# A mixture-of-experts stage from all experts on all tokens to three groups dense and five groups sorted by expert

## The chip, the cores and the metric

The kernel runs on one core of a Trainium2 chip. The metric is the device time of one execution in microseconds (us). All arithmetic of the path is in float32, except some counts in bf16.

## The reference

A decoder of two layers on x of 32 batches x 128 tokens x 128 channels, with a context of 32 x 77 x 128. The six blocks are the kernel's six stages; the third is the one that changes. Cut to what matters:

```python
x = x + _L0_attn_ref(_layernorm(x), ...)           # stage 1
x = x + _L0_xattn_ref(_layernorm(x), ctx, ...)     # stage 2
x = x + _L0_ffn_ref(_layernorm(x), ...)            # stage 3, below
x = x + _L1_attn_ref(_layernorm(x), ...)           # stage 4: 16 heads of 8, a bias by position
x = x + _L1_xattn_ref(_layernorm(x), ctx, ...)     # stage 5
x = x + _L1_ffn_ref(_layernorm(x), ...)            # stage 6: 16 experts, top 1

def _L0_ffn_ref(x, norm_weight, gate_w, w1, b1, w2, b2):     # 8 experts, hidden 256, top 2
    t = x * rsqrt(mean(x * x) + 1e-6) * norm_weight
    gate_logits = t @ gate_w.T
    gate_scores, expert_idx = top_k(gate_logits, 2)
    combine = zeros(T, 8).at[..., expert_idx].add(softmax(gate_scores))
    for W1, B1, W2, B2, c in experts:
        out += c[:, None] * (gelu(t @ W1.T + B1) @ W2.T + B2)
    return x + out
```

In the reference each expert is applied to every token, and six of the eight weights `c` of a token are zero.

## The kernel before

One program on the five engines, with semaphores written out by hand. Each stage has a function per engine (`by_tensor`, `by_vector`, `by_scalar`, `by_gpsimd`, `by_sync`), which issues that engine's instructions in a fixed order; an engine runs them in that order and waits where a `wait_ge` says so. x (`core.x`) stays in SBUF, tokens in the partitions. Batches are taken in groups of G = 4 (512 tokens); there are 8 groups. Stages overlap at their edges: a stage's `following` issues the next one's opening ("norm", "flip", "keys", "queries").

Stage three before is a loop over the groups (`turn(i, more)`), dense: for each group VectorE norms twice (a layer norm, then the RMS norm; `norm`, parts 1 to 4, spread between the experts of the group before), TensorE flips the tokens (L1857), computes logits (L1864), and then for each of 8 experts two hidden matmuls of 128 x 512 (L1872) and 8 output matmuls of 128 x 128 (L1880; each float32 matmul is two instructions in the trace). ScalarE applies GELU (L1732), VectorE adds the output times `combine` into `total` (L1833), and `route` finds the two best experts. GpSimd adds `total` to x (L1695). At its start GpSimd writes a tile of zeros (L1706), and SyncE clears a DRAM tensor of 16 regions x 4096 rows x 128 (`sorted_dram`, eight DMAs, L1676) which stage six uses.

Stage four is attention over the 32 batches, a software pipeline of one batch a step: TensorE scores (L1487), VectorE adds the bias (L1363) and takes the peak (L1377), GpSimd subtracts it (`lower`, L1199) and forms the keys by head for the next batch (`own_of`, L1190), ScalarE exponentiates (L1288), TensorE flips (L1498) and weighs (L1514), VectorE divides and adds to x. Every fourth step a new group is normalised: VectorE's moments (`moments_of`, which calls `before.x_of`), GpSimd's `rstd_of` (L1175 to L1184, with the power L1180), ScalarE's `xn_of` (L1246).

Stages five and six: `fourth_done` makes every engine wait, before stage five, for all of stage four's x and for `regions_cleared`. In stage six each token goes to one of 16 experts. During stage five `Routing` finds the expert and the rank of each token, and GpSimd writes the rows to the region of their expert in `sorted_dram` by indirect DMAs (L2642, 128 rows each). Then tiles of 128 rows of one expert are loaded by SyncE (L2794), flipped (L3039), multiplied with the weights of the tile's owner (L3053), whose number TensorE loads into a register, flipped (L3061), multiplied again (L3069), stored (L2804), and gathered by indirect DMAs (L2825). Four tiles are a quad.

## Time and profile before

| | |
|---|---|
| median of 3 runs | 1601.73 us (1600.66 to 1601.9) |
| the profiled execution | 1602.82 us, span 1601.0 us |
| TensorE busy | 94% of the span |
| VectorE, ScalarE, GpSimd busy | 60%, 52%, 37% |
| stage three (first logits to stage four's first queries) | 567.20 to 822.26 us |
| stage four's last x, start of stage five | 1047.94 us |

The span is from the first to the last instruction of the execution that was profiled; its own time is beside it. Busy times of engines overlap. A wait names the instruction that came last before it.

### The profile page before, as it was taken

To read this page: it belongs to the slowest core of one execution; us is meant where nothing else is said; L and a number is where in the kernel's file an instruction comes from. 1 tells how busy PE (TensorE), PEld (TensorE's weight loads), DVE (VectorE), ACT (ScalarE), POOL (GpSimd) and SP (SyncE) were. 2 spreads that over 40 slices of the span, in tenths; PEclk is the share of its full clock that TensorE was granted. 3 is DMA by queue.
4 is the path that set the end of the run, shared out by engine and by line. 5 is a ranking of instruction groups with operands and counts; after the bars stand their busy time and mean duration, and the time that the engine had idled before them with its cause. 6 is when DMAs were issued, how large, how long until landed. Compare 5 with 4: busy or idle time off the path is not lost.

```text
span 1601.0 us, 39392 instructions
## 1 busy us (share of the span) xinstructions
PE 1501.8 (94%) x15207; PEld 1146.3 (72%) x15207; DVE 959.2 (60%) x2605; ACT 832.8 (52%) x1574; POOL 588.7 (37%) x583
## 2 busy tenths in 40 slices
PE   6999999996999999999979999969999999998998
PEld 5777777765777767777756666647888888885765
DVE  3343444346788746655549999846666676675223
ACT  4545554445776634333347777625555655543431
POOL 4243445423222111111047878623333444444024
PEclk9999999998999999999999999979999999999999
DMA  5021230000000089400000000000000000000323
GB/s 153 16 61 29 73 108 7 12 1 5 11 10 6 7 303 384 153 0 0 0 1 2 2 2 2 2 12 2 6 6 8 11 13 7 9 7 31 97 74 88
DMA packets 76527, 68.85 MB, mean 43 GB/s; under 512 B 19533, under 2 KB 57034, under 8 KB 76234
## 3 DMA queue, kind: packets, MB, share of 16 engines
q1 hardware_dynamic: 74314, 62.36, 12.1%
q0 software_dynamic: 2048, 4.20, 0.8%
q8 instruction: 115, 1.88, 0.5%
q14 instruction: 50, 0.41, 0.1%
HBM read 24.58 MB, written 41.96 MB: 42 GB/s over the span
## 4 chain that ended last, share of the span: by engine, by line
PE 65%; issue 11%; POOL 10%; DVE 8%; ACT 4%; SPq 1%; DMA 1%; POOLq 0%; DVEq 0%; ACTq 0%
PE bank L1880 7%; PE bank L1872 7%; PE bank L2368 5%; PE bank L2400 5%; PE bank L2362 4%; PE bank L2379 4%; POOL s_p L1199 4%; PE bank L1498 3%; PE bank L1514 3%; PE bank L2391 3%; PE bank L853 2%; PE bank L3025 2%; PE bank L873 2%; PE bank L3014 2%; PE bank L826 2%
## 5 line engine op out<-in xcount | busy, mean ns | idle before, releaser
L1295 ACT COPY s_pT<-bank 77x512 f32<-77x512 f32 (+1 forms) x256 | 134.8, 585 | 71.7 <-PE bank L1498 71.4
L2190 POOL TENSOR_TENSOR s_p<-s_p,s_inverse 128x616 f32<-128x616 f32 x64 | 78.4, 1229 | 229.6 <-DVE s_inverse L2313 229.6
L1732 ACT ACTIVATE s_hT<-bank,w_s_b 128x512 f32<-128x512 f32 x128 | 87.3, 687 | 126.3 <-PE bank L1872 125.2
L1498 PE MATMUL bank<-ident,s_p 128*77 128x128 f32 (+1 forms) x1024 | 138.1, 281 | 12.3 <-ACT s_p L1288 10.5
L1498 PEld LDWEIGHTS bank<-ident,s_p 128*77 128x77 f32 (+1 forms) x1024 | 114.1, 146 | 40.2 <-ACT s_p L1288 22.5
L1880 PEld LDWEIGHTS bank<-w_s_w2T,s_hT 128*128 128x128 f32 x1024 | 122.3, 192 | 26.8 <-issue 15.3
L1199 POOL TENSOR_TENSOR s_p<-s_p,s_peak 128x1024 f32<-128x1024 f32 x64 | 120.1, 1898 | 30.2 <-DVE s_peak L1377 30.2
L1880 PE MATMUL bank<-w_s_w2T,s_hT 128*128 128x128 f32 x1024 | 124.4, 276 | 2.2 <-ACT s_hT L1732 2.2
L1288 ACT ACTIVATE s_p<-s_p 128x616 f32<-128x616 f32 (+1 forms) x128 | 111.4, 892 | 25.3 <-POOL s_p L1199 20.9
L1872 PE MATMUL bank<-s_ln_xnT,w_s_w1T 128*128 128x512 f32 x256 | 121.7, 604 | 0.0
L1833 DVE SCALAR_TENSOR_TENSOR s_total<-bank,s_combine,s_total 128x128 f32<-128x128 f32 x256 | 72.1, 344 | 74.6 <-PE bank L1880 73.2
L2297 DVE TENSOR_REDUCE s_peak<-bank 128x8 f32<-128x616 f32 x64 | 50.7, 792 | 88.4 <-PE bank L2379 88.4
L719 DVE TENSOR_TENSOR s_aT<-bank,s_weight 128x512 f32<-128x512 f32 x64 | 44.2, 691 | 98.7 <-PE bank L863 82.3
L2368 PE MATMUL bank<-pos_bias,s_ctx 128*32 128x128 f32 x3072 | 91.3, 274 | 0.6 <-issue 0.6
L2362 PE MATMUL bank<-s_ctx,s_kq 128*128 128x308 f32 x256 | 89.0, 440 | 1.9 <-ACT s_kT L2222 1.8
L2241 ACT ACTIVATE s_p<-s_p 128x616 f32<-128x616 f32 x64 | 46.6, 728 | 81.9 <-DVE s_p L2301 81.8
L1363 DVE TENSOR_TENSOR s_p<-bank,pos_bias 128x1024 f32<-128x1024 f32 x64 | 77.6, 1217 | 17.2 <-PE bank L1487 17.2
L2368 PEld LDWEIGHTS bank<-pos_bias,s_ctx 128*32 128x32 f32 x3072 | 82.1, 110 | 5.4 <-issue 1.6
L711 DVE TENSOR_TENSOR s_weight<-s_decay,bank 128x512 f32<-128x512 f32 x64 | 41.0, 682 | 73.4 <-ACT s_decay L559 73.4
L565 ACT COPY s_qT<-bank 128x512 f32<-128x512 f32 x64 | 37.5, 586 | 85.3 <-PE bank L826 85.3
L1190 POOL TENSOR_TENSOR w_s_q<-w_s_oT,w_s_lane_of 128x308 f32<-128x308 f32 (+1 forms) x64 | 55.2, 872 | 69.8 <-ACT w_s_oT L1261 32.3
L1487 PE MATMUL bank<-w_s_q,w_s_oT 32*128 32x308 f32 (+1 forms) x512 | 63.5, 566 | 16.2 <-POOL w_s_q L1190 12.5
(302 smaller groups left out, 3449.3 us busy)
## 6 DMA issues: line engine op xcount, KB each, us to landing
sorted_tokens<-s_zero SPq DMA_DIRECT2D x8, 4096.0 KB, 29.5
s_rows<-sorted_tokens SPq DMA_DIRECT2D x48, 64.0 KB, 1.9
routed_tokens<-s_routed SPq DMA_DIRECT2D x12, 256.0 KB, 2.4
x_all<-x SPq DMA_DIRECT2D x8, 256.0 KB, 3.1
w_s_gateup<-s_gateup SPq DMA_DIRECT2D x1, 2048.0 KB
out<-x_all SPq DMA_DIRECT2D x8, 256.0 KB
w_s_k<-ctxT SPq DMA_DIRECT2D x8, 154.0 KB, 2.2
s_ctx<-ctxT SPq DMA_DIRECT2D x8, 154.0 KB, 2.4
```

What stands on the lines that cost most here:

```text
L1199: nc.gpsimd.tensor_tensor(part, part, peak[:, b % 2, HU * u:HU * (u + 1)].unsqueeze(2).to_broadcast([P, HU, keys]), ALU.subtract).then_inc ...
L1288: nc.scalar.activation(part, part, ACT.Exp).then_inc(exp_ready, 1)
L1295: nc.scalar.copy(pT[0:keys, b % 2, 4 * q:4 * q + 4, :].rearrange("m h t -> m (h t)"), bank[0:keys, flip_bank("p", b, q), :]).then_inc(drai ...
L1363: nc.vector.tensor_tensor(p[:, b % 2, HU * u:HU * (u + 1), :].rearrange("p h m -> p (h m)"), scores_at(u).rearrange("p g c -> p (g c)"), b ...
L1498: last = nc.tensor.transpose(bank[0:keys, into, j * T:(j + 1) * T], p[:, b % 2, 4 * q + j, :], core.ident[:, :])
L1732: nc.scalar.activation(hT[:, e % 2, c, :], bank[:, HIDDEN + k % 4, :], ACT.Gelu, bias=w.s3_b1[:, k:k + 1]).then_inc(hT_ready, 1)
L1872: nc.tensor.matmul(bank[:, HIDDEN + k % 4, :], w.s3_w1T[:, k * P:(k + 1) * P], ln.xnT[:, :], start=True, stop=True).then_inc(hidden_done, 1)
L1880: last = nc.tensor.matmul(bank[:, OUT[e % 2], n * D:(n + 1) * D], hT[:, e % 2, c, n * T:(n + 1) * T], w.s3_w2T[:, e * CHUNKS + c, :], star ...
L2190: nc.gpsimd.tensor_tensor(part, part, inverse[:, b % 2, heads].unsqueeze(2).to_broadcast([P, HU, M]), ALU.mult).then_inc(share_ready, 1)
L2362: nc.tensor.matmul(bank[:, into, 0:GM].rearrange("p (n m) -> p n m", m=M), kq[:, h, :], ctx[:, g % 3, :, 0:M], start=True, stop=True).then ...
L2368: last = nc.tensor.matmul(bank[lane:lane + LANE, into, tile * D:(tile + 1) * D], ctx[:, g % 3, b % G, row:row + LANE], vo[:, QUAD * q + he ...
L2400: last = nc.tensor.matmul(bank[:, OUT, 0:D], pT[:, b % 2, j, :], values(b, j // PER_QUAD)[:, j % PER_QUAD, :], start=(j == 0), stop=(j == ...
```

## The change

Stage three is written anew. Groups 0, 1 and 2 (`DENSE`) are computed as before, by all eight experts, in 24 units of one expert on one group, `UNITS3`. The tokens of groups 3 to 7 go to two experts each. The routing of all groups runs beside the 24 units: `STARTS3` says at which unit a group starts, and its phases follow slot by slot (0 moments and scales, 1 norm, 2 flip, 3 logits, 4 route, 5 combine or count of rows ahead, 6 offset or rank, 7 to 10 dispatch). A count by matmul gives each row its rank; GpSimd writes each token's row twice, by indirect DMAs, into the regions of its two experts in DRAM (40 DMAs of 128 rows). VectorE's `settle` works out once where the tiles of each expert stand. Then 48 tiles (12 quads) of rows of one expert are loaded, flipped, multiplied with W1 as the moving operand and the rows stationary, biased on VectorE (`add_biases`, b1 spread over all partitions), passed through GELU on ScalarE, flipped (8 flips a quad), multiplied with W2, biased (`keep_routed`) and stored. In stage four GpSimd gathers two rows for each token (`gather`, 40 indirect DMAs in steps 3 to 22), and VectorE multiplies them by the token's shares and adds them to x (`add_results`, eight instructions a group, inside `moments_of`).

The norms are also new: one set of moments gives the scales of both norms (GpSimd, `scales_of`), and ScalarE writes the tokens and replaces x by x plus its layer norm (`normalise`, eight activations a group), so that only the experts' sum is added later. Where the regions are cleared is changed too: at the start only the 8 x 2560 rows of stage three, and the whole of `sorted_dram` again, for stage six, once stage four's gathers have landed. Stage six's semaphores for dispatch and gather are fewer, its work is the same.

```diff
...
+                before.gather(pool, b)
...
+DENSE = 3
+SORTED = GROUPS - DENSE
+TILES3 = SORTED * G * 2 + E3
+QUADS3 = TILES3 // G
+REGION3 = SORTED * GT
+CLEARINGS3 = 4
+FLIGHTS = 4
+TOKENS = 6
+UNITS3 = DENSE * E3
+STARTS3 = {3: 0, 1: 1, 4: 3, 5: 5, 6: 7, 7: 9, 2: 10}
+ORDER3 = [0] + sorted(STARTS3, key=lambda g: STARTS3[g])
+COUNTED, SETTLED = 14, 15
...
     def by_sync(sp):
         sp.wait_ge(zero_ready, 1)
+        cleared_rows = sorted_dram[0:E3 * REGION3, :].rearrange("(k p j) d -> k p (j d)", p=P, k=CLEARINGS3)
+        for k in range(CLEARINGS3):
+            sp.dma_start(cleared_rows[k].rearrange("p (r c) -> p r c", c=GT),
+                         zero[:, :].unsqueeze(1).to_broadcast([P, E3 * REGION3 * D // CLEARINGS3 // P // GT, GT])
+                         ).then_inc(cleared, 16)
+        sp.wait_ge(gap_ready, 1)
+        for tile, source in ((b1_all, a["s3_b1"]), (b2_all, a["s3_b2"].rearrange("e d -> (e d)"))):
+            sp.dma_start(tile[:, :], source.unsqueeze(0).to_broadcast(tile.shape)).then_inc(biases_landed, 16)
+        def load(q):
+            for n in range(q * G, (q + 1) * G, 2):
+                pair = nc.sync.value_load(pairs_index[0:1, n // 2:n // 2 + 1], min_val=0, max_val=ALL_ROWS ** 2 - 1)
+                for k, tile in enumerate((pair & (ALL_ROWS - 1), pair >> ALL_ROWS.bit_length() - 1)):
+                    sp.dma_start(rows[:, (n + k) % (FLIGHTS * G), :],
+                                 tiles_dram[bass.ds(tile & (ALL_ROWS - 1), 1), :, :].rearrange("k p d -> p (k d)")
+                                 ).then_inc(rows_landed[q % FLIGHTS], 16)
+        sp.wait_ge(pairs_ready, 1)
+        for g in range(DENSE, GROUPS):
+            sp.wait_ge(dispatched[g - DENSE], G * 2 * 16)
+        for g in range(DENSE):
+            sp.wait_ge(filled, turn["xnT", g] + 1)
+        for q in range(FLIGHTS):
+            load(q)
+        for q in range(QUADS3):
+            if q + FLIGHTS < QUADS3:
+                sp.wait_ge(filled, turn["rows", q] + 1)
+                load(q + FLIGHTS)
+            sp.wait_ge(out_used, UNITS3 + q + 1)
+            sp.dma_start(done_dram[q * GT:(q + 1) * GT, :].rearrange("(n p) d -> p n d", p=P),
+                         routed[:, q % 2, :, :]).then_inc(routed_stored[q % 2], 16)
...
+        for k in range(2):
+            sp.wait_ge(gathered[k], (SORTED + 1 - k) // 2 * G * 2 * 16)
         cleared_rows = sorted_dram.rearrange("(k p j) d -> k p (j d)", p=P, k=CLEARINGS)
         for k in range(CLEARINGS):
             sp.dma_start(cleared_rows[k].rearrange("p (r c) -> p r c", c=GT),
...
+        def dispatch(g, n):
+            b = (g - DENSE) * G + n
+            if n == 0:
+                if g == DENSE:
+                    pool.wait_ge(cleared, CLEARINGS3 * 16)
+                pool.wait_ge(ranking_v, ranked_links(g) + RANKED)
+                pool.wait_ge(tokens_ready, G * (nth(g) + 1))
+            for k in range(2):
+                nc.gpsimd.indirect_dma_start(
+                    out=sorted_dram[:, :], out_offset=bass.IndirectOffsetOnAxis(ap=slot_index[:, b, k:k + 1], axis=0),
+                    in_=tokens_of(g)[:, n, :], in_offset=None).then_inc(dispatched[g - DENSE], 16)
...
+        for k in range(UNITS3):
+            if group_in(k, 0) is not None:
+                scales_of(group_in(k, 0))
+            for n in range(G):
+                if group_in(k, 7 + n) in range(DENSE, GROUPS):
+                    dispatch(group_in(k, 7 + n), n)
+            if k % E3 == 1 and k > E3:
+                add_total(k // E3 - 1)
+        add_total(DENSE - 1)
+        following.by_gpsimd(pool, "norm")
+        following.by_gpsimd(pool, "keys")
...
+    def gather(pool, step):
+        g, n = (step + 9) // G, (step + 9) % G
+        if g not in range(DENSE, GROUPS):
+            return
+        j, b = g - DENSE, (g - DENSE) * G + n
+        if (j, n) == (0, 0):
+            pool.wait_ge(done_ready, 1)
+            for k in range(2):
+                pool.wait_ge(routed_stored[k], QUADS3 // 2 * 16)
+        if j >= 2 and n == 0:
+            pool.wait_ge(added, 2 * (j - 1))
+        for k in range(2):
+            nc.gpsimd.indirect_dma_start(
+                out=rows[:, j % 2 * 2 * G + 2 * n + k, :], out_offset=None, in_=done_dram[:, :],
+                in_offset=bass.IndirectOffsetOnAxis(ap=done_index[:, b, k:k + 1], axis=0)).then_inc(gathered[j % 2], 16)
+    def add_results(dve, g):
+        j = g - DENSE
+        dve.wait_ge(gathered[j % 2], (j // 2 + 1) * G * 2 * 16)
+        dve.wait_ge(x_normed, GROUPS)
+        for k in range(2):
+            if k:
+                dve.wait_ge(added, 2 * j + 1)
+            for n in range(G):
+                x = core.x[:, g * G + n, :]
+                last = nc.vector.scalar_tensor_tensor(
+                    out=x, in0=rows[:, j % 2 * 2 * G + 2 * n + k, :], scalar=share[:, g * G + n, k:k + 1], in1=x,
+                    op0=ALU.mult, op1=ALU.add)
+            last.then_inc(added, 1)
+        dve.wait_ge(added, 2 * j + 2)
...
+        def normalise(g):
+            i = nth(g)
+            act.wait_ge(shifts_ready, i + 1)
+            if i >= TOKENS:
+                earlier_g = ORDER3[i - TOKENS]
+                act.wait_ge(filled, turn["xnT", earlier_g] + 1)
+                if earlier_g >= DENSE:
+                    act.wait_ge(dispatched[earlier_g - DENSE], G * 2 * 16)
+            for n in range(G):
+                nc.scalar.activation(tokens_of(g)[:, n, :], core.x[:, g * G + n, :], ACT.Identity,
+                                     bias=shifts[:, i % 2, 1, n:n + 1],
+                                     scale=scales[:, i % 2, 1, n:n + 1]).then_inc(tokens_ready, 1)
+            act.wait_ge(tokens_ready, G * (i + 1))
+            for n in range(G):
+                x = core.x[:, g * G + n, :]
+                last = nc.scalar.activation(x, x, ACT.Identity, bias=shifts[:, i % 2, 0, n:n + 1],
+                                            scale=kept[:, i % 2, n:n + 1])
+            last.then_inc(x_normed, 1)
...
+        def output_of_tiles(q, owned):
+            u = UNITS3 + q
+            pe.wait_ge(drained, turn["hidden", q, CHUNKS - 1] + 1)
+            pe.wait_ge(out_used, u - 1)
+            for n in range(G):
+                for c in range(CHUNKS):
+                    last = nc.tensor.matmul(bank[:, OUT[u % 2], n * D:(n + 1) * D], hT[:, u % 2, c, n * T:(n + 1) * T],
+                                            w.s3_w2T[:, bass.ds(owned[n] * CHUNKS + c, 1), :], start=(c == 0),
                                             stop=(c == CHUNKS - 1))
             last.then_inc(expert_done, 1)
...
+        for k in range(UNITS3):
+            if group_in(k, 2) is not None:
+                flip_tokens(group_in(k, 2))
+            if group_in(k, 3) is not None:
+                logits_of(group_in(k, 3))
+            if group_in(k, 5) is not None:
+                (flip_combine if group_in(k, 5) < DENSE else count_ahead)(group_in(k, 5))
+            if k == COUNTED:
+                count_all()
+            if k == 0:
+                hidden_of(0)
+            if k + 1 < UNITS3:
+                hidden_of(k + 1)
+            if group_in(k, 6) in range(DENSE):
+                offset_of(group_in(k, 6))
+            output_of(k)
+        pe.wait_ge(owners_ready, 1)
+        flip_rows(0)
+        flip_rows(1)
+        now = owners_of(0)
+        hidden_of_tiles(0, now)
+        for q in range(QUADS3):
+            if q + 1 < QUADS3:
+                later = owners_of(q + 1)
+                hidden_of_tiles(q + 1, later)
+            if q + 2 < QUADS3:
+                flip_rows(q + 2)
+            if q:
+                output_of_tiles(q - 1, past)
+            if q == QUADS3 - 1:
+                following.by_tensor(pe, "opened")
+            flip_hidden(q)
+            if q == QUADS3 - 2:
+                core.wait_set_back(pe)
+                pe.wait_ge(drained, turn["hidden", q, CHUNKS - 1] + 1)
+                following.by_tensor(pe, "flip")
+                following.by_tensor(pe, "keys")
+            past, now = now, later
+        output_of_tiles(QUADS3 - 1, past)
+        pe.wait_ge(out_used, UNITS3 + QUADS3 - 1)
+        following.by_tensor(pe, "queries")
...
```

`x_of(engine, g)` of stage three waits for `x_ready` in groups 0 to 2 and calls `add_results` in the others. `QUADS3` is 12.

## Rows read from the trace of the kernel before

**Rows 1.** The page: busy us, share of the span, instructions of each engine.
```profile
PE 1501.8 (94%) x15207; PEld 1146.3 (72%) x15207; DVE 959.2 (60%) x2605; ACT 832.8 (52%) x1574; POOL 588.7 (37%) x583
```
**Rows 2.** Timeline of TensorE in stage three: start us, us, what [idle before].
```profile
567.20 1.87 PE L1864 MATMUL bank<-w_s_gateT,s_ln_xnT 128*128 128x8 f32 x8 [0.77 <-ACT s_ln_xnT L1716]
...
601.13 0.96 PE L1864 MATMUL bank<-w_s_gateT,s_ln_xnT 128*128 128x8 f32 x8
...
621.19 1.95 PE L1880 MATMUL bank<-w_s_w2T,s_hT 128*128 128x128 f32 x16
...
624.69 1.95 PE L1880 MATMUL bank<-w_s_w2T,s_hT 128*128 128x128 f32 x16
...
632.20 0.96 PE L1864 MATMUL bank<-w_s_gateT,s_ln_xnT 128*128 128x8 f32 x8
...
822.26 1.02 PE L1468 MATMUL bank<-w_s_v,w_s_q 128*128 128x512 f32 x2
```
**Rows 3.** Busy time in a stretch of stage four: PE, PEld, DVE, ACT, POOL.
```profile
900.00:940.00 40.00, 37.51 (x558) 26.23 (x557) 37.86 (x61) 29.14 (x48) 31.18 (x26) 1.00 0.01 2
```
**Rows 4.** Timeline of GpSimd in stage four and at its end.
```profile
880.84 1.01 POOL L1180 TENSOR_TENSOR s_rstd<-s_variance,minus_half 128x4 f32<-128x4 f32 x1
...
896.02 3.75 POOL L1199 TENSOR_TENSOR s_p<-s_p,s_peak 128x1024 f32<-128x1024 f32 x2 [2.31 <-DVE s_peak L1377]
902.39 1.04 POOL L1190 TENSOR_TENSOR w_s_q<-w_s_oT,w_s_lane_of 128x512 f32<-128x512 f32 x1 [2.62 <-ACT w_s_oT L1261]
...
976.12 3.75 POOL L1199 TENSOR_TENSOR s_p<-s_p,s_peak 128x1024 f32<-128x1024 f32 x2 [2.32 <-DVE s_peak L1377]
...
1047.94 1.06 POOL L2124 MEMSET s_ctx<- 128x1152 f32 x1 [8.86 <-DVE x_all L1403]
```
**Rows 5.** Timeline of TensorE in stage six: counts of rows ahead, then a quad.
```profile
1459.83 0.22 PE L2695 MATMUL bank<-s_chosen,s_ones 128*128 128x48 bf16 x3
...
1498.67 1.89 PE L3053 MATMUL bank<-w_s_gateup,s_rowsT 128*128 x8
1500.40 0.60 PE L3039 MATMUL bank<-ident,s_rows 128*128 128x128 f32 x4
1500.84 1.06 PE L3069 MATMUL bank<-w_s_down,s_hiddenT 128*128 x8
...
1502.17 1.89 PE L3053 MATMUL bank<-w_s_gateup,s_rowsT 128*128 x8
```
**Rows 6.** Timeline of ScalarE: the norm's activations of a group of four.
```profile
803.48 1.65 ACT L1246 ACTIVATE w_s_v<-x_all,s_shift,s_rstd 128x128 f32<-128x128 f32 x4 [6.75 <-POOL s_shift L1184]
```
**Rows 7.** VectorE's busy time in three stretches: route, rank, moments of a group.
```profile
602.46:605.03 2.57, 2.43 (x20) 1.00 1.03 386
1461.24:1462.12 0.88, 0.77 (x5) 1.00 0.00 0
613.80:615.14 1.34, 1.30 (x10) 1.00 1.03 388
```
**Rows 8.** Timeline of SyncE in stage six: two stores, four loads between them.
```profile
1503.29 0.42 SPq L2804 DMA_DIRECT2D routed_tokens<-s_routed  x1
...
1508.11 0.43 SPq L2804 DMA_DIRECT2D routed_tokens<-s_routed  x1
```
**Rows 9.** The line of the indirect DMAs: ns min/median/max, first and last start.
```profile
L2642 POOL DMA_INDIRECT sorted_tokens<-w_s_oT,s_slot_index x32: 953/1057/1215, 1234.8 to 1472.7; - x32
```
**Rows 10.** Timeline of GpSimd: the gap from one indirect DMA to the next.
```profile
1470.17 0.96 POOL L2642 DMA_INDIRECT sorted_tokens<-w_s_oT,s_slot_index  x1 [0.30 <-issue]
```
**Rows 11.** The page's DMA issues: count, KB each, median us to landing.
```profile
sorted_tokens<-s_zero SPq DMA_DIRECT2D x8, 4096.0 KB, 29.5
```
**Rows 12.** A stretch in stage three: busy times, clock, DMA share, GB/s.
```profile
580.00:600.00 20.00, 20.00 (x124) 15.22 (x124) 12.09 (x55) 7.45 (x11) 2.42 (x4) 1.00 1.03 383
```
**Rows 13.** Timeline of VectorE: eight multiply-adds of 128 x 128.
```profile
611.60 2.29 DVE L1833 SCALAR_TENSOR_TENSOR s_total<-bank,s_combine,s_total 128x128 f32<-128x128 f32 x8
```
**Rows 14.** A line of GpSimd in stage one, a sum of 128 x 512: ns min/median/max.
```profile
L510 POOL TENSOR_TENSOR s_z<-s_z,w_s_b x8: 1265/1688/1697, 83.8 to 368.6; 128x512 f32<-128x512 f32 x8
```

More of the change, by code:

```diff
@@ new lines, in by_scalar @@
+        keep_rows(0)
+        keep_rows(1)
+        gelu_of_tiles(0)
+        for q in range(QUADS3):
+            if q + 2 < QUADS3:
+                keep_rows(q + 2)
+            if q + 1 < QUADS3:
+                gelu_of_tiles(q + 1)
+            keep_hidden(q)
+            if q == 6:
+                core.wait_set_back(act)
+                following.by_scalar(act, "norm")
+            if q == QUADS3 - 2:
+                following.by_scalar(act, "flip")
+                following.by_scalar(act, "keys")
@@ L1796, in route, with link @@
             for n in range(G):
+                last = nc.vector.bn_aggr(moments[:, i % 2, n, :], stats[:, n, :])
+            last.then_inc(moments_ready, 1)
+        def route(g):
+            links = routed_links(g)
+            def link(instruction):
+                nonlocal links
+                links += 1
+                instruction.then_inc(routing_v, 1)
+                dve.wait_ge(routing_v, links)
+            batches = slice(g * G, (g + 1) * G)
+            dve.wait_ge(drained, turn["logits", g] + 1)
+            for n in range(G):
@@ L1958, in stage3, with x_of @@
+    def x_of(engine, g):
+        if g < DENSE:
+            engine.wait_ge(x_ready, g + 1)
+        else:
+            add_results(engine, g)
+    LAST = UNITS3 + QUADS3
+    after = After(x_of=x_of, memory=lambda engine: engine.wait_ge(core.set_back, 1),
+                  score_banks=lambda pe: pe.wait_ge(biased, QUADS3),
+                  work_bank=lambda pe: pe.wait_ge(out_used, LAST), gather=gather)
     return Opening(None, by_gpsimd, by_scalar, by_vector, by_tensor, main), after
```

804 lines of the change are left out of this document (544 added, 260 removed).

## The prediction

> **What bounds the kernel now.** I read the page first, then the waits, then the timelines of TensorE, VectorE, ScalarE and GpSimd in stages three, four and six. TensorE is busy for 94% of the span and no other engine for more than 60% [rows 1]. That average hides two regimes.
>
> Stage three runs from its first logits at 567.20 to the first query projection of stage four at 822.26, 255.1 us [rows 2]. It is TensorE work laid end to end: a group of four batches takes 632.20 - 601.13 = 31.07 us, an expert 624.69 - 621.19 = 3.50 us. So eight experts take 28.0, and flips, logits and offset 3.07.
>
> Stage four is different. TensorE and VectorE are both about 94% busy and GpSimd 78% [rows 3], but the chain goes again and again through GpSimd's `lower`. Four steps take (976.12 - 896.02) / 3 = 26.7 us. GpSimd's own work in them is 4 x 3.75 for `lower`, 4 x 1.04 for `own` and 1.6 for the norm of which the power is 1.01, about 20.7 us; the rest of 26.7, 6.0, it waits, 2.3 and 2.6 of it at one `lower` and one `own` [rows 4]. That slack is what the change spends.
>
> **Stage three after: the dense part.** 24 units instead of 64: 24 x 3.50 = 84.0. Three whole groups add 3 x 3.07 = 9.2. The other five still need a flip (0.44, [rows 5]), logits (about 0.8 of the 0.96 shown in [rows 2]), and a count of rows ahead, whose five small bf16 matmuls get 0.2 (three take 0.22 in stage six [rows 5]): 7.2. The pipe's filling, now in the 6.5 us that 255.1 has over eight groups, gets 2.0. Together 102.4.
>
> To this come stalls, as each engine now does a group every two slots. ScalarE takes the norms over: 8 activations a group, four in 1.65 us [rows 6], behind the GELUs of the slot, while TensorE's next slot opens with the flip of these very tokens. Laid out slot by slot, the flip is late by 1.7 and 1.2 us for the first two groups (an offset copy stands ahead there) and by 0.5 for the next three. For group 7, VectorE has route, rank and moments in one slot, of which today's forms take 2.6, 0.9 and 1.3 us [rows 7]; then GpSimd's scales, with a power over twice the columns of today's 1.01, about 2.7 in all: 2.3 late. Group 2 is the eighth to be normalised and there are six token buffers, so its norm waits until all dispatches of group 3 have landed, and these stand in GpSimd's queue behind the scales of groups 6, 7 and 2. The last lands some 19 us after slot 9 starts; TensorE wants the flip at 14.5 and the tokens take 1.65 more: 6.2 late. Sum 12.9, so the dense part is 115.3; 102.4 if none is exposed.
>
> VectorE needs 6.0 and 1.2 us in two slots of some 8.7, so it follows. `settle`, once, is covered by the two output banks.
>
> **The sorted part.** 5 x 4 x 2 + 8 = 48 tiles, 12 quads. Stage six has the same pipeline and prices the steps: a quad takes 1502.17 - 1498.67 = 3.50 us, of it 1.73 for four tile matmuls of 256 columns, 0.44 for a flip of four, 0.89 for the output [rows 5]. Here the output has two chunks (1.78) and the hidden flip is twice as long (0.88): 1.73 + 0.44 + 1.78 + 0.88 = 4.83, times 12: 58.0. SyncE issues four loads and a store in 1508.11 - 1503.29 = 4.8 us [rows 8]: as much, so it may set the pace by a little. VectorE needs about 2.2 for eight adds and as much for register work, which no row of before shows on VectorE. I take the TensorE figure; with VectorE or SyncE as the bound I allow 5.2 to 6.0, that is 4 to 14 us more.
>
> Entry: GpSimd has 20 pairs of dispatches. An indirect DMA takes 0.95 to 1.22 us [rows 9]; I take 1.03, and 0.30 until the next [rows 10], a pair 2.6. Sixteen pairs are left some 17 us after slot 9; they end near 60, and with landing and two quads' loads the rows are there at 71, where TensorE would be ready at 67.5: 3 us, then 1.5 for the copy of the rows and 0.8 for the first biased hidden, and 2.4 at the exit. 7.7 together. With the flip and keys of stage four, 1.3, stage three is 115.3 + 58.0 + 7.7 + 1.3 = 182.3: **72.8 saved**. Bounds: 89 (no stall in either part) and 55 (quads of 6.0, indirect DMAs of 1.5).
>
> The small clearing (10.5 MB) starts at GpSimd's memset in the tail of stage two and at 383 GB/s [rows 12] takes 27 us: it is over before the first dispatch. The two bias broadcasts run behind it unseen.
>
> **Stage four: the gathers.** Two indirect DMAs follow `lower` in each of steps 3 to 22. Behind them in GpSimd's queue stand the next `own`, for which the scores wait, and the next `lower`, for which the exponentials wait. Four steps then hold 20.7 + 8 x 1.33 = 31.3 us of GpSimd's work against 26.7: the 6.0 of waiting is used up and 4.6 is left, five times: **23**. The least is 5 x (8 x 1.25 - 6.0) = 20; the most, with no waiting used, 53. I stay near the least, since the gathers fall where GpSimd waits now. VectorE gets eight more multiply-adds in four steps, 2.3 us [rows 13], on 25.2 of 26.7; beside 31.3 they are covered, except after step 23, where no gather is left: 1.5. Sum 24.5.
>
> **From stage four to five: the clearing.** The eight DMAs of 4096 KB [rows 11] move. They ran at the start of stage three beside the experts; at 383 GB/s, all 16 engines full [rows 12], 33.6 MB take 87.6 us, with start and landing 88.9. Now SyncE issues them only when the last gather, that of step 22, has landed, and every engine enters stage five only when they are complete. In the trace `lower` of step 22 ends at 979.87 and stage five begins at 1047.94 [rows 4], 68.1 later. After the change the pair takes 2.7 of issue and lands 2.3 later, so the clearing ends 5.0 + 88.9 = 93.9 after that `lower`; the stage ends 68.1 + 2.7 + 1.5 = 72.3 after it. All engines stand for **22** us (17 to 26). By the Trainium skill (DMA: Bandwidth & Descriptors, Specifications) a core gets some 358 GB/s of HBM, which would make the clearing 94 us, an estimate, and the wait 28; the trace's 383 is above that and decides.
>
> **Sum.** -72.8 + 24.5 + 22 = -26.3. The profiled execution took 1602.82 us beside its span of 1601.0, so 1576.5; the median of the runs is 1601.73, 1.1 lower: **1575 us**. 0.2%, 3 us, is what a measurement can tell from no change.
>
> **Rivals.**
> - *Stage three without the stalls* (0.15). ScalarE uses some 7.5 of 8.7 us in two slots, so there is room if the shifts come early. -89 + 24.5 + 22 = -42.5: 1559. Against it: the six buffers are a fixed wait behind a full queue.
> - *The wait before stage five does not show* (0.07). -48.3: 1553. It needs a last gather 22 us earlier or a tail of stage four that much longer, and the rate in [rows 12] speaks against it.
> - *VectorE's adds hold GpSimd up* (0.14). The 40 multiply-adds of the gathered rows read two tiles in SBUF while GpSimd lowers scores. If GpSimd stands still for all of them, 5 x 2.3 = 11 us more: 1587. This would be the rule of the Trainium skill (GPSIMD Engine Reference, Specifications): GpSimd's SBUF interfaces are shared with VectorE, with contention when a VectorE instruction has two SBUF inputs. In this trace one and the same GpSimd sum takes 1.27 us at the least and 1.69 in the median [rows 14], so something of the kind may be real.
> - *Slower: the indirect DMA costs more under load* (0.12). The rows are of a GpSimd with little beside it. Each microsecond more for one costs 40 us in stage four, and 32 in stage three, where the dispatches already end last: 72. From 26.3 / 72 = 0.37 us more, 1.70 for each, the gain is gone; at 1.8 the time is 1609. The longest in the trace, 1.22 and the gap of 0.30 [rows 9, 10], would give 1588.
> - The forecast itself has 0.52, its own range 1563 to 1589.
>
> The range 1556 to 1598 leaves out the hidden wait below and the slower case above, 2 in 10. Faster 0.85, within 0.2% 0.03, slower 0.12.
>
> **What will show it.** Dense slots with a gap of about 6 us at the flip of group 2; quads of 4.8 to 5.2 us; stage three near 182 us. In stage four, four steps in 31 us with GpSimd above 95% busy for steps 3 to 22, then 26.7 again. A hole of some 22 us on all engines ahead of stage five's folding, with DMA at 383 GB/s under it. Wrong would be: quads above 6 us (register work on VectorE), GpSimd still idle between gathers, or indirect DMAs above 1.5 us.

## The result and the profile after

The changed kernel took 1609.16 us in the median of five runs (1606.01 to 1611.02), the kernel before 1601.9 beside it (1600.66 to 1604.11). The ratio is 1.0043, 95% interval 1.0028 to 1.0058: slower, where 1575 had been forecast. The profiled execution took 1611.02 us with a span of 1609.1, against 1602.82 and 1601.0: 8.1 more, where 26.3 less was expected.

The page of the kernel after: the engines, and the chain that ended last.
```profile
PE 1445.7 (90%) x14805; PEld 1111.7 (69%) x14805; DVE 928.6 (58%) x2414; ACT 835.0 (52%) x1618; POOL 662.8 (41%) x678
...
PE 59%; issue 14%; DVE 10%; POOL 7%; ACT 6%; DMA 1%; another core or an unknown queue 1%; SPq 1%; DVEq 0%; POOLq 0%; ACTq 0%
```
TensorE has 56 us less to do than in [rows 1], but stands still for 64 us more, and 14% of the chain (11% before) is "issue", time in which nothing that the profile shows was waited for. The timeline of TensorE in the dense part, the sorted part and at stage four's first queries shows where:
```profile
569.05 1.85 PE L2294 MATMUL bank<-w_s_gateT,s_dense_xnT 128*128 128x8 f32 x8 [0.43 <-DVE x_all L1404]
...
629.86 1.39 PE L2287 MATMUL bank<-ident,s_tokens 128*128 128x128 f32 x4 [1.05 <-ACT s_tokens L1963]
...
643.49 1.54 PE L2287 MATMUL bank<-ident,s_tokens 128*128 128x128 f32 x4 [8.73 <-ACT s_tokens L1963]
...
646.96 3.76 PE L2345 MATMUL bank<-s_dense_xnT,w_s_w1T 128*128 128x512 f32 x4
...
669.90 0.94 PE L2357 MATMUL bank<-w_s_w2T,s_hT 128*128 128x128 f32 x6
671.77 0.27 PE L2357 MATMUL bank<-w_s_w2T,s_hT 128*128 128x128 f32 x1 [0.93 <-issue]
...
675.32 0.37 PE L2357 MATMUL bank<-w_s_w2T,s_hT 128*128 128x128 f32 x1 [1.04 <-issue]
...
682.40 0.81 PE L2357 MATMUL bank<-w_s_w2T,s_hT 128*128 128x128 f32 x3 [1.76 <-issue]
...
707.08 1.04 PE L2365 MATMUL bank<-ident,s_tokens 128*128 128x128 f32 x8
...
719.91 1.89 PE L2380 MATMUL bank<-w_s_w1T,s_rowsT 128*128 x8
...
724.74 1.89 PE L2380 MATMUL bank<-w_s_w1T,s_rowsT 128*128 x8
...
772.49 1.02 PE L1469 MATMUL bank<-w_s_v,w_s_q 128*128 128x512 f32 x2
```
Stage three takes 772.49 - 569.05 = 203.4 us, 51.7 less than in [rows 2] where 72.8 was forecast. The dense part, up to the flip of rows at 707.08, takes 138.0 for 115.3; the sorted part 65.4 for 67.0, its quads 4.83 us to the hundredth. Group 2's flip waits 8.7 us, and the four matmuls at 646.96 take 3.76 us behind it instead of 1.88: the granted clock is 0.50 there, TensorE's lower level (1.2 GHz), after it had stood still. Then comes something that no step of the prediction had, called the hole below: from 670 to 683 us the output matmuls come one in about 1.4 us. The profile names "issue" as the releaser, which means that it shows nothing waited for. The two stretches (TensorE, its weight loads, VectorE, ScalarE, GpSimd, granted clock, DMA share, GB/s):
```profile
644.00:648.00 4.00, 3.73 (x18) 2.75 (x18) 0.00 (x0) 2.97 (x9) 3.09 (x4) 0.50 0.18 55
...
670.00:683.00 13.00, 4.12 (x16) 3.34 (x17) 2.00 (x8) 0.34 (x1) 7.41 (x8) 0.57 0.15 45
```
In the hole only GpSimd works. ScalarE stands too, though the matmuls that release its copy are recorded as done at 669.97 (668.82 and 1.15, in TensorE's timeline):
```profile
682.66 0.58 ACT L2006 COPY s_total<-bank 128x512 f32<-128x512 f32 x1 [13.73 <-remote]
```
"remote" says that the profile found no release near its start. GpSimd's timeline, the first and the last of sixteen dispatches that follow each other without a pause:
```profile
659.64 0.96 POOL L1882 DMA_INDIRECT sorted_tokens<-s_tokens,s_slot_index  x1 [5.94 <-DVE s_slot_index L2163]
...
678.59 0.96 POOL L1882 DMA_INDIRECT sorted_tokens<-s_tokens,s_slot_index  x1 [0.30 <-issue]
```
Stage four runs from 772.49 to its last output and then waits; SyncE's timeline and a stretch beside it show for what (TensorE's rows first, of before and of after):
```profile
1047.07 0.49 PE L1524 MATMUL bank<-w_s_o,s_oT 128*128 128x128 f32 x2 [1.40 <-DVE s_oT L1395]
1049.69 0.50 PE L2152 MATMUL bank<-w_s_qT,w_s_kT 64*128 64x128 f32 x4 [2.14 <-DVE w_s_o L2134]
```
```profile
1033.22 0.49 PE L1525 MATMUL bank<-w_s_o,s_oT 128*128 128x128 f32 x2 [1.40 <-DVE s_oT L1396]
1056.62 0.80 PE L2697 MATMUL bank<-w_s_qT,w_s_kT 64*128 64x128 f32 x4 [22.91 <-DVE w_s_o L2679]
```
```profile
965.07 71.44 SPq L1846 DMA_DIRECT2D sorted_tokens<-s_zero  x8
```
```profile
1040.00:1050.00 10.00, 0.00 (x0) 0.00 (x0) 0.00 (x0) 0.00 (x0) 0.00 (x0) 0.50 1.03 389
```
From the first queries to the last output it was 1047.07 - 822.26 = 224.8 us and is 260.7: 35.9 more, forecast 24.5. From there to stage five's folding it was 2.6 and is 23.4: the wait for the clearing is 20.8 us, forecast 22. The opening is 1.8 us later, the rest about 1. So -51.7 + 35.9 + 20.8 + 1.8 + 1.3 = +8.1.

Two questions for the experiments: what fills the 23 us of the dense part that were not forecast, and why stage four pays 36. In stage four VectorE's eight additions for a group stand in a block, beside GpSimd's lowering:
```profile
865.92 3.80 POOL L1199 TENSOR_TENSOR s_p<-s_p,s_peak 128x1024 f32<-128x1024 f32 x2
```
```profile
867.61 2.25 DVE L1947 SCALAR_TENSOR_TENSOR x_all<-s_tokens,s_share,x_all 128x128 f32<-128x128 f32 x2 [0.17 <-DMA s_tokens<-routed_tokens,s_done_index]
```
```profile
L1947 DVE SCALAR_TENSOR_TENSOR x_all<-s_tokens,s_share,x_all x40: 339/347/1981, 834.4 to 969.8; 128x128 f32<-128x128 f32 x40
```
Most of the forty take 0.35 us (minimum, median, maximum in ns), but one in each block takes 1.98. The second of the two shown ends at 869.86, 0.14 behind GpSimd's sum.

### The profile page after: what moved, and what is told of

Its sections match the earlier page's. It is cut to its first block, busy times and chain, and to the rows that moved or that the text cites. A ratio compares the mean times of both kernels' runs of the same rounds, so it can differ in the third digit from the quotient of the medians.

```text
span 1609.1 us, 38896 instructions
## 1 busy us (share of the span) xinstructions
PE 1445.7 (90%) x14805; PEld 1111.7 (69%) x14805; DVE 928.6 (58%) x2414; ACT 835.0 (52%) x1618; POOL 662.8 (41%) x678
## 3 DMA queue, kind: packets, MB, share of 16 engines
q1 hardware_dynamic: 93034, 80.71, 15.5%
## 4 chain that ended last, share of the span: by engine, by line
PE 59%; issue 14%; DVE 10%; POOL 7%; ACT 6%; DMA 1%; another core or an unknown queue 1%; SPq 1%; DVEq 0%; POOLq 0%; ACTq 0%
PE bank L2913 5%; PE bank L2945 5%; PE bank L1515 5%; PE bank L1499 4%; PE bank L2907 4%; PE bank L2924 4%; PE bank L2936 3%; PE bank L853 2%; PE bank L3566 2%; PE bank L873 2%; POOL s_p L1199 2%; PE bank L3555 2%; PE bank L826 2%; PE bank L2345 2%; PE bank L3557 2%
## 5 line engine op out<-in xcount | busy, mean ns | idle before, releaser
L1499 PE MATMUL bank<-ident,s_p 128*77 128x128 f32 (+1 forms) x1024 | 141.5, 285 | 14.5 <-ACT s_p L1289 10.6
L1515 PE MATMUL bank<-s_pT,s_v 77*32 77x128 f32 (+1 forms) x2048 | 73.6, 287 | 21.5 <-DVE x_all L1404 20.4
L1515 PEld LDWEIGHTS bank<-s_pT,s_v 77*32 77x32 f32 (+1 forms) x2048 | 55.8, 114 | 44.6 <-issue 32.5
L1515 PE MATMUL bank<-s_pT,s_ones 77*32 77x128 f32 (+1 forms) x2048 | 78.5, 285 | 2.9 <-issue 2.8
L2924 PE MATMUL bank<-s_kT,s_xnT 128*128 128x308 f32 x256 | 72.9, 426 | 5.9 <-ACT s_xnT L2760 5.4
L853 PEld LDWEIGHTS bank<-s_level,w_band 128*128 128x128 f32 x512 | 59.6, 191 | 26.2 <-issue 19.7
```

The costliest lines, as they stand in the source:

```text
L853: last = nc.tensor.matmul(bank[:, LEVEL + j, c * H1 * TB:(c + 1) * H1 * TB], w.band[:, start:start + T], level[:, b % 2, a, :, :].rearrang ...
L1499: last = nc.tensor.transpose(bank[0:keys, into, j * T:(j + 1) * T], p[:, b % 2, 4 * q + j, :], core.ident[:, :])
L1515: last = nc.tensor.matmul(bank[LANE * r:LANE * (r + 1), WORK, at_column:at_column + T], of_lane(r, j), pT[0:keys, b % 2, LANES * r + j, :] ...
L2924: last = nc.tensor.matmul(bank[:, SCORE5 + q, 0:QUAD * M].rearrange("p (h m) -> p h m", m=M), xnT[:, n * T:(n + 1) * T], kT[:, g % 2, QUAD ...
```

## The experiments

Kernels that leave work out (e4, e6 to e8, e13, e14, e17) and the repeats e15 and e18 ran once each. The kernel before, run beside every set, took 1600.2 to 1601.7 us in the median wherever it ran.

**The clearing moved (e1, e2).** Stage three gets a DRAM tensor of its own, so the clearing for stage six waits for nothing.
```diff
+    sorted3_dram = nc.dram_tensor("sorted_tokens3", [E6 * REGION, D], F32, kind="Internal").ap()
...
-        for k in range(2):
-            sp.wait_ge(gathered[k], (SORTED + 1 - k) // 2 * G * 2 * 16)
-        cleared_rows = sorted_dram.rearrange("(k p j) d -> k p (j d)", p=P, k=CLEARINGS)
+        cleared_rows = later_dram.rearrange("(k p j) d -> k p (j d)", p=P, k=CLEARINGS)
```
e1 issues it behind stage three's last store, e2 behind the bias broadcasts, beside the dense part.

> Stage three gets a sorted tensor of its own in DRAM; the eight clearing DMAs of the tensor of stage six (33.6 MB) no longer wait for the gathers and are issued behind stage three's last store, near 773 us. Theory one (the 21 us in which every engine stands before stage five are this transfer's place in the order, and nothing else waits there): the folding of stage five starts some 21 us earlier, span 1609 - 21 = 1588, if the gathers (64 KB each, from 796 us on) are not held up by the transfer beside them. Rival A: the gathers share the 16 DMA engines with the transfer until about 860; each then lands several us later, GpSimd or VectorE wait for them, and 5 to 10 us of the gain are lost: 1593 to 1598. Rival B: the wait before stage five has another cause, and the time stays at 1609.

> As e1_own_late, but the eight DMAs are issued right behind the two bias broadcasts, near 585 us, so that they run beside the dense part until about 675. Theory one: the wait before stage five goes, 1588, but the dispatches (from 618 us on, 64 KB each) share the DMA engines with the transfer; if they land late, the token buffers of group 2 and SyncE's first loads come later. I expect 0 to 5 us of loss, 1588 to 1593. Rival: the unforeseen hole in TensorE near 670 to 683 us is a lack of instructions whose fetch queues behind DMA traffic; then the hole grows to 20 us or more or comes earlier, stage three takes 210 us or more, and the time is 1595 to 1605. If DMA traffic has nothing to do with it, the hole keeps its 12.5 us.

e1 took 1591.56 us (1582.84 to 1594.78; ratio 0.9933, 0.9904 to 0.9962), e2 1594.24 (0.9957, 0.9943 to 0.9971). In e1's timeline of TensorE the folding follows stage four as before the change:
```profile
1033.52 0.49 PE L1525 MATMUL bank<-w_s_o,s_oT 128*128 128x128 f32 x2 [1.40 <-DVE s_oT L1396]
1036.14 0.81 PE L2695 MATMUL bank<-w_s_qT,w_s_kT 64*128 64x128 f32 x4 [2.14 <-DVE w_s_o L2677]
```
The wait is that transfer's place in the order and nothing else. The gain in time is 17.6 us against the changed kernel's 1609.16, and 21.2 between the two profiles. A little of rival A is there too: with the transfer beside it (e1, e10 to e12, e16) stage four takes 261.4 to 262.7 us, in the four profiles of the changed kernel 258.4 to 260.7. For e2 a stretch beside the transfer, and the hole:
```profile
600.00:640.00 40.00, 31.99 (x198) 23.22 (x196) 25.64 (x157) 24.04 (x57) 21.88 (x36) 0.95 1.04 385
...
670.00:683.00 13.00, 4.78 (x20) 3.53 (x19) 2.00 (x9) 0.12 (x1) 7.67 (x8) 0.64 0.19 60
```
The DMA engines were full until about 670 us, TensorE went on, and the hole came when they were free; it kept its length. What grew is group 2's wait, 12.7 us for 8.7: dispatches land later beside a full transfer.

**A seventh token buffer (e3).**
```diff
-TOKENS = 6
+TOKENS = 7
-    passed_by = sbuf("passed_by", [P, G, 2, E3])
+    passed_by = shared_out
```


> Seven token buffers instead of six (an intermediate of 256 bytes is shared to make room): group 2's tokens no longer wait until all of group 3's dispatches have landed. Theory one: the 8.7 us before the flip of group 2 go, and with them most of the 3 us that slow matmuls take behind it; stage three takes 203.4 - 11 = 192, the time is 1598. Rival: GpSimd's queue (scales of groups 7 and 2 behind dispatches) holds group 2 nearly as long, so 2 us at most are gained: 1607. For the hole: if it hangs on the dispatches it stays near the last sixteen of them; if on a place in TensorE's program, it stays at the output of the same unit.

1611.79 us (1.0064, 1.0047 to 1.0081): nothing gained, though the wait it aims at has gone. TensorE:
```profile
635.53 1.54 PE L2287 MATMUL bank<-ident,s_tokens 128*128 128x128 f32 x4 [1.79 <-ACT s_tokens L1963]
...
669.77 0.27 PE L2357 MATMUL bank<-w_s_w2T,s_hT 128*128 128x128 f32 x1 [0.94 <-issue]
```
Group 2's flip is 8 us earlier and waits 1.8 instead of 8.7. Two waits of 2.3 and 2.7 us take its place near 651 and 655, with four matmuls at half speed behind the second, and the hole begins 1.2 us earlier, counted from the first logits. The second wait is for ScalarE's copy of the logits:
```profile
654.34 0.19 ACT L1984 COPY s_logits<-bank 128x32 f32<-128x32 f32 x1 [10.85 <-remote]
```
What that copy needs had been done by 648.8 us (the logits' matmuls by 645.7, VectorE's search in the earlier logits by 648.8). It starts 5.5 us later, 1.6 us after fourteen dispatches without a pause, 635.2 to 652.7, have ended. So it looks as if TensorE, let through by the buffer, ran into the same hold one row of dispatches earlier. e10 and e16, the other kernels with seven buffers, show the same copy with 10.36 and 11.57 us "remote"; none of the three ran on a chip without the hole. The sorted part starts at 704.67, 2.4 earlier, and takes 1.3 longer. Both theories missed: the buffer frees the wait, and the time is lost again before GpSimd is through.

**No dispatches (e4).** The forty indirect DMAs and the waits on them are left out; the tiles read cleared rows.
```diff
             for k in range(2):
-                nc.gpsimd.indirect_dma_start(
-                    out=sorted_dram[:, :], out_offset=bass.IndirectOffsetOnAxis(ap=slot_index[:, b, k:k + 1], axis=0),
-                    in_=tokens_of(g)[:, n, :], in_offset=None).then_inc(dispatched[g - DENSE], 16)
```

> GpSimd's forty dispatches of stage three are left out (the tiles are read from the cleared tensor, so the routed results are those of zeros); all else stays. Theory one (the hole of 12.5 us on TensorE near 670 us comes from the indirect DMAs back to back on GpSimd): the hole goes, as do the 8.7 us before the flip of group 2; the dense part takes 138 - 12.5 - 11 = 114.5 us, near the 115.3 forecast, and the time is 1585 or so. Rival: the hole is of TensorE's own instruction supply at that place of its program, or of the work of settling on VectorE; then it stays, the dense part takes some 127, and the time is 1597.

1588.36 us. The stretch, and the end of the dense part on TensorE:
```profile
670.00:683.00 13.00, 13.00 (x83) 10.08 (x82) 3.83 (x14) 4.95 (x8) 0.00 (x0) 1.00 0.11 30
```
```profile
684.13 1.04 PE L2358 MATMUL bank<-ident,s_tokens 128*128 128x128 f32 x8
```
No hole, no wait of group 2: the dense part takes 684.13 - 569.85 = 114.3 us. So both are the dispatches' doing, and stage three as a whole, 180.1 us, is near the 182.3 forecast. VectorE's settling is still there.

**Paced and plain dispatches (e5, e6).** e5 waits for TensorE's progress before a pair; e6 issues plain DMAs of the same bytes.
```diff
+                    pool.wait_ge(expert_done, k)
                     dispatch(group_in(k, 7 + n), n)
```
```diff
-                nc.gpsimd.indirect_dma_start(
...
+                row = (2 * b + k) * P
+                nc.gpsimd.dma_start(sorted_dram[row:row + P, :], tokens_of(g)[:, n, :]).then_inc(dispatched[g - DENSE], 16)
```


> As the changed kernel, but GpSimd waits before the pair of dispatches of a slot until TensorE has finished that slot's number of experts, so at most one pair goes out in about 3.5 us instead of one in 2.5. Theory (TensorE's signals are held up while GpSimd issues indirect DMAs without a pause for longer than some 9 to 14 us): the hole of 12.5 us near 670 us goes or shrinks below 4 us; TensorE is through with the dense part near 695, the last dispatch comes later than before, near 700, and the sorted part starts near 710: about the same total, 1605 to 1612, with the time now in the wait for rows. Rival A (the number of dispatches, not their spacing, holds TensorE up): the hole keeps its length, 1615 or more. Rival B (the place in TensorE's program): the hole stays at the output of the seventeenth unit.

> Each indirect dispatch is replaced by a plain DMA on GpSimd's queue with the same source and the same 64 KB, to rows that lie together (so the routed results are not the reference's). Theory one (the hold comes from GpSimd's own work of making 128 descriptors for each indirect DMA): no hole, the dense part takes about 115 us as without dispatches, 1588. Rival (the traffic of 64 KB transfers and their completions holds TensorE's signals): the hole stays, with a dense part above 125 us.

**Gathers without adds, adds without gathers (e7, e8).** e7 puts a tiny copy in the place of a block of adds; e8's `gather` returns at once.
```diff
-                last = nc.vector.scalar_tensor_tensor(
-                    out=x, in0=rows[:, j % 2 * 2 * G + 2 * n + k, :], scalar=share[:, g * G + n, k:k + 1], in1=x,
-                    op0=ALU.mult, op1=ALU.add)
-            last.then_inc(added, 1)
+            nc.vector.tensor_copy(core.spare[:, :], core.minus_half[:, 0:1]).then_inc(added, 1)
```
```diff
-        if g not in range(DENSE, GROUPS):
-            return
+        return
```

> The 40 multiply-adds of the gathered rows on VectorE are left out, the gathers stay (x lacks the routed results of five groups). Theory one (GpSimd's queue bounds a group of four steps in stage four, the adds only add a little over 2 us to it): four steps take 31 us instead of 33.6, stage four is 12 us shorter than the 261 of the changed kernel. Rival (the adds are covered and the gathers alone cost the 36 us): four steps stay at 33.6.

> The 40 gathers are left out, the adds stay and read what lies in the buffers. Theory one: GpSimd has its 6 us of waiting per four steps back, the adds (2.3 us) go on VectorE, which was busy for 94%: four steps take 27 to 29 us instead of 33.6 and stage four some 235 us instead of 261. Rival (the adds with two SBUF inputs slow GpSimd's lower down as much as the gathers do): four steps stay above 30 us.

e5 took 1602.06 us (1.0002, 0.9992 to 1.0012), e6 1590.45, e7 1589.28, e8 1597.13. None had the hole; e7 and e8 were not meant to lose it, since their stage three is the changed kernel's, so e5 and e6 prove nothing of it yet. In e5 the pacing did not even part the last sixteen dispatches, which follow each other from 659.36 to 679.53 as before: TensorE was ahead of what GpSimd waited for. For stage four they speak clearly. Four steps of e7, then of e8 (columns as above):
```profile
849.42:880.16 30.74, 26.73 (x381) 19.37 (x377) 25.39 (x40) 19.66 (x32) 28.37 (x25) 0.94 0.07 19
```
```profile
921.29:954.28 32.99, 27.89 (x376) 20.40 (x377) 29.70 (x46) 19.55 (x32) 20.62 (x17) 0.91 0.05 20
```
With gathers alone four steps take 30.74 us for 26.7 in [rows 4]; with adds alone 32.0 to 33.1; with both 32.5 to 33.6. The whole stage takes 245.2, 254.0 and 260.7 us for 224.8: gathers alone cost 20.4, adds alone 29.2, both 35.9 (e13 and e14, the same kernels again, 245.8 and 253.8). I had expected the adds to be the small part. In e8, GpSimd's and VectorE's timelines:
```profile
880.79 3.80 POOL L1199 TENSOR_TENSOR s_p<-s_p,s_peak 128x1024 f32<-128x1024 f32 x2
881.75 4.69 DVE L1944 SCALAR_TENSOR_TENSOR x_all<-s_tokens,s_share,x_all 128x128 f32<-128x128 f32 x8
...
887.91 0.19 POOL L1175 TENSOR_SCALAR s_minus_mean<-s_moments 128x4 f32<-128x4 f32 x1 [3.31 <-DVE s_moments L1355]
```
The block takes 4.7 us instead of 8 x 0.29 = 2.3 [rows 13]; behind it come the moments, for which GpSimd waits 3.3 us here, and the next scores. VectorE is busy for 90% of these four steps, so I read it as a delay of the chain rather than a load on VectorE; how the 29.2 us divide was not measured.

**The changed kernel again (e9), and combinations (e10 to e12).** e10 is e1 with e3's buffer. e11 is e1 with the adds spread, two in each step; e12 adds the pacing of e5.
```diff
                 add_bias(step, 1)
+                before.add(dve, step)
                 peak_of(step, 0)
```


> The changed kernel once more, unaltered, beside the kernels of this call. Of the profiles so far the hole of some 12 us on TensorE stands in the changed kernel and in e1 to e3, and not in e5, e7 and e8, though e7 and e8 have the same stage three to the instruction. Theory one (the hole is a matter of the execution or of the chip, not of the program): this profile may lack it; then the dense part takes 123 to 126 us and the span is near 1597. Rival (the hole belongs to how this program lies in memory or to a timing that the edits of e5, e7 and e8 shift): it stands again near 670 us and the time is 1609 as before.

> The clearing as in e1 (own tensor, issued behind stage three's last store) and seven token buffers as in e3. If group 2's wait of 8.7 us is worth what it shows, and the hole is apart from it: e1 - 8, 1583; with the gain of e3 eaten up again as there, 1591. If the hole is absent, 1573 to 1578.

> The clearing as in e1, and the adds of stage four spread: one batch (two multiply-adds) in the middle of a step, behind the addition of the bias and ahead of the peaks, instead of eight in a block ahead of the moments, where two of them run into GpSimd's lowering and one takes 1.98 us instead of 0.35. Theory: a group of four steps falls from 33.1 to about 31 us, near the 30.75 of e7 without adds; stage four is 10 us shorter, so 1591.6 - 10 = 1582. Rival (each pair of adds delays the peaks, on which GpSimd's lowering waits, and GpSimd is the bound): four steps stay at 33, 1590.

> e11 with the dispatches paced as in e5. If pacing is what removes the hole, stage three takes 196 us as in e5 and the time is 7 us below e11, 1575; if the hole's absence in e5 was chance, both have it or lack it alike and e12 is within 2 us of e11, or slower by the later dispatches.

e9 1612.12 us (1.0067, 1.0050 to 1.0084), e10 1592.25 (0.9940, 0.9916 to 0.9964), e11 1589.80 (0.9933, 0.9916 to 0.9950), e12 1584.10 (0.9884, 0.9867 to 0.9900). e9, e10 and e11 have the hole. The stretch of e12:
```profile
670.00:683.00 13.00, 10.81 (x59) 7.09 (x57) 5.17 (x20) 4.21 (x7) 9.61 (x10) 1.00 0.14 42
```
On this chip, where three other kernels had the hole, pacing leaves short stops (the longest 2.2 us); stage three takes 196.8 us against 203.7 in e11. On GpSimd the row of fourteen dispatches is parted into ten and four by 4.3 us, the row of sixteen into twice eight by 2.0, and the last four by 1.1; the pauses of 5.2 and 5.4 us that e11 has between its rows shrink to 1.2 and 1.5. The time, 1584.1, is not the 1575 expected. e10 shows no more than e1: the seventh buffer is again worth nothing beside the hole. Spreading the adds gained nothing: stage four is 262.6 us in e11 and 262.7 in e1. An add of e11, on VectorE:
```profile
884.87 1.41 DVE L1943 SCALAR_TENSOR_TENSOR x_all<-s_tokens,s_share,x_all 128x128 f32<-128x128 f32 x1
```
and GpSimd's work in that moment:
```profile
885.07 1.05 POOL L1190 TENSOR_TENSOR w_s_q<-w_s_oT,w_s_lane_of 128x512 f32<-128x512 f32 x1
```
Of eight adds above 0.5 us in e11, four meet the queries' sum and take 1.41 to 1.73, and four still meet the lowering. The rival's 1590 came; that it came by delayed peaks, as the rival had it, is not shown.

**Does the hole go with the program or the chip (e13 to e18)?** e13 and e14 are e7's and e8's kernels again, e15 and e18 the changed kernel, e16 is e1 with seven buffers and paced dispatches, e17 is e6's kernel.

> e7's kernel again (the 40 multiply-adds of gathered rows left out). If the hole near 670 us goes with the program and its place in memory, it is absent again: dense part 123 us, span 1587. If its absence in e7 was the chip's or the execution's, it is there: dense part 136, span 1600.

> e8's kernel again (the 40 gathers left out). As for e13: absent and 1595 if it goes with the program, there and 1608 if with the chip or the execution.

> The changed kernel a third time, the control for this chip: with the hole 1610, dense part 137; without it 1597, dense part 124. If it lacks the hole here, the chip decides; if it has it and e13 and e14 lack it, the program does.

> Own tensor with the early clearing (e1), seven token buffers (e3) and paced dispatches (e5), the adds in a block. From e5's 1602: minus 21 for the clearing, 1581; the seventh buffer takes the 8.4 us before group 2's flip, but the paced dispatches end last, so 0 to 5 us more: 1576 to 1581. Rival (the buffers and pacing bring new waits for rows): 1584 or more.

> e6's kernel again (plain DMAs of the same 64 KB from the same queue in place of the forty indirect dispatches; routed results are not the reference's). If the hole comes from GpSimd making the descriptors of indirect DMAs back to back, it is absent while e18 has it: TensorE busy for all of 660 to 673 us, dense part 119 us. If it comes from the transfers or their completions, it is there too, dense part 130 us or more.

> The changed kernel as control for e17's chip. With the hole near 670 us and a dense part of 134 to 138 us, e17 says something; without it, e17 does not.

On the chip of e1 to e4 e13 took 1597.76 us, e14 1603.36 and e15 1606.98, all with the hole (dense parts 137.2, 134.9, 134.6); e16 1584.30 (0.9901, 0.9883 to 0.9919), with short stops only, the rival's time for 1576 to 1581 expected. Buffer and pacing together are no better than pacing and spread adds in e12. On the next chip e17 took 1594.70 and e18 1599.79. The stretch and the end of the dense part in e18, the unaltered changed kernel:
```profile
670.00:683.00 13.00, 13.00 (x74) 9.17 (x73) 5.71 (x22) 5.42 (x9) 10.38 (x11) 1.00 0.17 52
```
```profile
693.44 0.60 PE L2365 MATMUL bank<-ident,s_tokens 128*128 128x128 f32 x4
696.27 0.88 PE L2365 MATMUL bank<-ident,s_tokens 128*128 128x128 f32 x4 [2.23 <-DMA s_tokens<-sorted_tokens]
```
Same program, no hole: dense part 123.9 us, stage three 192.8, span 1598.0. By then TensorE waits 2.2 us for rows, so GpSimd's queue is the next bound, and the hole is worth the 7 to 12 us that lie between this run and the changed kernel's others (1606.98 to 1612.12), with the reserve that it ran once. Of the four chips whose number is on record, kernels with unpaced indirect dispatches had the hole on two in nine of nine profiles (e1 to e3 and e13 to e15; e9 to e11) and on the other two in none of three (e7, e8; e18). e5 makes it none of four, its last sixteen dispatches being as close as the others'. Where the hole is absent pacing costs rather than gains: stage three takes 196.5 us in e5 and 192.4 and 192.5 in e7 and e8 on the same chip. e17's lack of the hole says as little as e6's: whether the making of descriptors or their transfers hold TensorE up stays open. Their plain dispatches do shorten group 2's wait to 4.0 us, and the dense part to 119.4 and 119.6. e2 speaks against the mere load on the DMA engines: 60 GB/s in its hole, 385 before it.

## Why the prediction was wrong

The direction was wrong by 34 us: -26.3 forecast, +8.1 measured.

**The sorted part was right.** 12 quads of 4.83 us, neither SyncE nor VectorE the bound, 65.4 us for 67.0. The indirect DMA cost 0.96 and 0.30 between two, as in [rows 9, 10]; the rival that it is dearer under load, the only one that ended slower, has no part in the result, although its 1609 was the time that came.

**The wait for the clearing was right**, 20.8 us for 22, and e1 shows it whole. The trace decided against 358 GB/s (the Trainium skill, DMA: Bandwidth & Descriptors, Specifications): with every engine standing it ran at 389 GB/s, and at 385 beside the dense part in e2.

**The dense part failed at the stalls**, 12.9 us forecast and 138.0 - 102.4 = 35.6 measured. Without any dispatch the part takes 114.3 (e4), with them 123.9 (e18), with the hole 134 to 138. So the 22.7 us that were missed fall into three.
- 5.2: without group 2's wait the forecast was 102.4 + 12.9 - 6.2 = 109.1, and e4 took 114.3. That 114.3 lies near the forecast's 115.3 is luck. The forecast priced all matmuls by rows at the full clock; in e4 eight hidden matmuls at 571.55 took 6.68 us for 2 x 1.88 = 3.76, and four at 632.33 took 3.54 for 1.88. For these 4.6 us it had only the 2.0 of filling.
- 3.4: from 114.3 to 123.9 is the term "six token buffers" in kind, 9.6 for 6.2. The flip was late by 8.7, and the matmuls behind it ran at the lower clock.
- 14.1: from 123.9 to 138.0 is the hole, no term at all: an engine that waits on nothing that the profile shows. The prediction lets GpSimd's dispatches cost TensorE nothing but the waits for rows and buffers. No row of before has sixteen indirect DMAs in a row beside a busy TensorE, so it could not be priced from them; but the range could have been wider for a pattern that the trace had never run.

These are differences of single profiles, e18's from another chip. What makes the hold is open.

**Stage four failed at the adds.** The gathers were priced at 23 and cost 20.4 alone. The adds were "covered", 1.5 us; on top of the gathers they cost 260.7 - 245.2 = 15.5. Two things were wrong. Their duration came from a row with one operand in PSUM [rows 13], and the rival that named the contention had the wrong victim: it let GpSimd stand still for VectorE. The trace shows the reverse: the add that meets GpSimd's sum takes 1.98 us, and ends just behind it, while GpSimd's lowerings keep their time (1896/1898/1902 ns before, 1887/1897/1946 after, minimum, median, maximum). By the Trainium skill (SBUF — State Buffer, the section on its two separate sides) GpSimd and a VectorE instruction with two SBUF inputs take a shared port pair as an exclusive lock, and the second to start is blocked until the first ends. The trace agrees on who waits, 1.98 for 0.35 us, in stage four as changed; in e11 it does not agree on the order, for an add recorded as starting 0.20 us ahead of GpSimd's sum (884.87, 885.07) still ends behind it. And a group's eight adds stand ahead of its moments, on the chain: work that would fit into an engine's idle share is not covered if the next thing on the path stands behind it.

**Sum of the misses:** dense part +22.7, sorted part -1.6, stage four +11.4, clearing -1.2, opening and the rest +3.1: 34.4.

**What beats both kernels.** e12 and e16, 1584 us, 1.0 to 1.2% below the kernel before. The moved clearing does most of it, pacing some 6 us more where the hole is (e12 against e11). Both were measured only on chips that have the hole.

## To carry to other kernels

A transfer that shares a buffer with the stage before takes over that stage's end: give it a tensor of its own before counting what the new stage saves. Price an operation by a row with the same kinds of operands and the same neighbour at work, and ask what stands directly behind it, not how idle its engine is. When one stall is removed (e3) and nothing is gained, follow every engine that stands to what it needs, and compare when that was done with when it went on: in e3 that shows ScalarE held up during an earlier row of dispatches. And run the same program again on another chip before an edit is credited with a change.

## What the runs showed of the hardware

- With sixteen indirect DMAs issued back to back (one in 1.26 us, 128 rows of 512 bytes), TensorE's matmuls came one in 1.4 us for some 12 us, beginning 10 to 12 us after the first and ending about 3 us after the last. ScalarE's copy of the offset, released by a matmul recorded at 669.9, started at 682.66. It happened on some chips only: same program, dense part 123.9 us on one and 134.6 to 138.0 on others. Fourteen in a row (e3) came with a ScalarE copy 5.5 us late, 1.6 us after the last had ended. Pauses of 4.3, 2.0 and 1.1 us inside the rows removed most of it (e12). The mechanism is open.
- A VectorE multiply-add of 128 x 128 with both tensors in SBUF takes 0.35 us, 1.98 when it meets a GpSimd sum of 128 x 1024 (1.90) and 1.41 beside one of 128 x 512 (1.05): it ends some 0.15 us behind the sum, and the sum keeps its time.
- Behind 8.7 us of waiting, TensorE's granted clock was 0.50 (1.2 GHz) over 644 to 648 us, and four hidden matmuls took 3.76 us instead of 1.88.
- Writes of zeros to DRAM ran at 383 to 385 GB/s with all 16 DMA engines full, beside compute, and at 389 with nothing else running.
